# Cross-attention and FFN on one core: FFN rows laid out by DMA in the head, x2 ahead of q's third pair on GpSimd and ahead of q's last sum on VectorE

## The chip, the cores and the metric

One core of one Trainium2 chip. The metric is the device time of one execution of the kernel in microseconds; the profile is of one execution. TensorE multiplies matrices and transposes tiles into PSUM; VectorE, ScalarE and GpSimd work element by element; SyncE and the queues issue DMAs. Each engine works off its own instructions in the order in which they are written and waits on semaphores for the others.

## The reference

The input x has 16 batches of 128 x 1024 (channels x tokens), and so has ctx. Both stages add to x:

```python
def _layernorm(x, axis=-1, eps=1e-05): ...          # over the 1024 tokens
# cross attention, 8 heads of 64, q from layernorm(x), k and v from ctx
qh = softmax(Wq q, axis=-2) * SCALE                 # over the 64 of a head
kh = softmax(Wk k, axis=-1)                         # over the tokens
context = einsum('bhdn,bhen->bhde', kh, vh)
out = Wo (context qh) + bo
x = x + out / max(norm(out), 1e-12) * g * sqrt(128)
# FFN, 4-bit weights: low and high nibble of qweight, per output scale and zero
w = (w_int - round(zeros / scales)) * scales
x = x + layernorm(x) w + bias
```

The result is x after both, in float32.

## The kernel before

The weights are prepared once, then 16 batches go through a software pipeline. `iteration(i, ...)` is written once for every engine; in it, batch n = i + 1 is loaded, normalised and given k's first projection, batch a = i goes through q and k (attention weights), batch c = i - 1 through the attention's output and its norm (up to x2, the sum after the first stage), and batch f = i - 2 through the FFN. Iterations -1 (FIRST) to 2 are peeled, which also hold the set-up, 3 to 14 are a hardware loop with two iterations to a turn (ScalarE's ends earlier), 15 (END) to 17 are peeled again. An iteration has eight steps j. The order of an engine's work is the order of the `if j == ...` lines by hand; nothing is planned at run time.

The names that matter:

- TensorE: `project_q(j)` makes q for 128 tokens in one PSUM bank (three matmuls, `ps_q`), `project_k(b, j)` k for 128 of 512 rows in two banks (`ps_k`), `transpose_k`, `transpose_c` turn k's exponentials and ctx, `mix_m` is k times ctx (fp32), `mix_g` multiplies with the product of Wv and Wo (`vo`), `mix_out(h)` makes the attention output of half h from g and the turned q, `feed_forward` the FFN, whose last matmul adds zero and bias rows from `ffn_rows`. `set_up_cols` and `set_up_row` spread scales, zeros and bias over the partitions by 3 + 24 transposes in iteration 0.
- VectorE: `max_k` (L840, the k maximum), `shift_q` (L847 maximum, L852 shift), `sum_q(a, p)` (L859, L862: sum and reciprocal of the pair p of q's eight slices), `stats2` and its mean (L1046, L1052), `split_g` (L887, L892: g's high and low part), `low_x2`, `attend`, `fit_g`, whose last instruction is `gs_undo` (L879). In the head it also picks the nibbles of the packed weights (`set_up_late`, L830, one per step j of iteration 0) and mixes and splits the rows (L795 to L806) in iteration 1.
- ScalarE: `exp_q`, `exp_k(b, sums, j)` (L558), `high_q(b, p)` (L574, the f16 high part of pair p), `move_m` (L602), `normalise_x2` (L638), `high_x2` (L647), `xn_hi` (L744), `convert_nibble` (L535), `squares`. At step 0 it issues the loads of x_res, x and ctx (L693 to L700).
- GpSimd: `scale_q(b, p)` (L417, L419), `low_q(b, p)` (L429, what is left of q after the high part), `c_lo`, `xn_lo` (L499), the sum x2 (L510), `fit_x2` (L442 to L447: x2's rstd and mean times rstd), `add_y`.
- SyncE: it turns each finished q part and x2 part by DMA transpose, in the order of the code (`turn_q`, L347, L372, L377), each behind a wait.

The FFN's x2 comes into TensorE's layout by the transposes of x2n_hi and x2n_lo. The order around the change: on GpSimd at step 6 `scale_q(a, 2)`, at step 7 `xn_lo`, x2, `low_q(a, 2)`; at step 0 of the next iteration `fit_x2(f)`, `scale_q(c, 3)`, `low_q(c, 3)`. On VectorE at step 7: q's shift, `max_k(n, 0)`, `sum_q(a, 3)`, x2's statistics, k's reciprocal, the mean. On ScalarE at step 0: `move_m`, the load issues, `normalise_x2`, `exp_q(0)`, `high_x2`, `high_q(c, 3)`, `exp_k(a, s, 1)`.

## Time and profile before

| what | value |
| --- | --- |
| time, median of 3 runs | 705.52 us (703.21 to 708.35) |
| the profiled execution | 706.99 us, its span 704.9 us |
| TensorE busy | 654.4 us, 93% of the span |
| VectorE busy | 555.5 us, 79% |
| GpSimd busy | 474.5 us, 67% |
| ScalarE busy | 449.6 us, 64% |
| mean granted TensorE clock | 0.978 |

Times in the rows are us from the start of the span; a line number is that of the code above. A bracket at the end of a timeline row is the idle time of the engine ahead of the instruction and what ended it. TensorE's matmuls overlap, so their durations add up to more than the time between their starts.

### The profile page before, as it was taken

How to read it: one execution, taken by the hardware profiler on the slowest of the kernel's cores; microseconds unless marked ns; L12 is line 12 of the kernel's file. 1: busy time of each engine (PE TensorE's matmuls, PEld its weight loads, DVE VectorE, ACT ScalarE, POOL GpSimd, SP SyncE). 2: the span in 40 equal slices, each digit the busy share in tenths (PEclk: the TensorE clock that was granted, in tenths of full speed). 3: DMA queues.
4: the chain of work that ended last, by engine and by line, in shares of the span. 5: the costliest groups of instructions: out<-in, count | busy, mean ns of one | idle time of the engine just before them, and what ended most of it. 6: DMA issues, size and time to landing. Idle time of an engine off the chain costs nothing.

```text
span 704.9 us, 11155 instructions
## 1 busy us (share of the span) xinstructions
PE 654.4 (93%) x3312; PEld 420.1 (60%) x3328; DVE 555.5 (79%) x900; ACT 449.6 (64%) x747; POOL 474.5 (67%) x406
## 2 busy tenths in 40 slices
PE   4858799999999999999999999999999999999987
PEld 3635556666666666656666666666666665666543
DVE  2997778888878788888878888888878887887844
ACT  3575666767585767667485666758575766748432
POOL 2166286776949496785949677694949678594820
PEclk9989889999999999999999999999999999999989
DMA  8125236363553637263454636255363724344451
GB/s 297 62 52 120 54 54 171 91 152 59 149 113 83 164 89 179 50 173 74 119 126 96 166 89 163 50 154 105 80 161 89 179 53 116 69 114 78 92 106 60
DMA packets 178871, 78.43 MB, mean 111 GB/s; under 512 B 168328, under 2 KB 169888, under 8 KB 178848
## 3 DMA queue, kind: packets, MB, share of 16 engines
q1 hardware_dynamic: 172512, 55.09, 36.9%
q10 hardware_dynamic: 6336, 23.07, 9.7%
q8 instruction: 10, 0.16, 0.1%
q14 instruction: 13, 0.11, 0.1%
HBM read 28.32 MB, written 8.39 MB: 52 GB/s over the span
## 4 chain that ended last, share of the span: by engine, by line
PE 34%; POOL 25%; issue 19%; DVE 12%; ACT 7%; DMA 1%; POOLq 0%; another core or an unknown queue 0%; DVEq 0%; ACTq 0%; SPq 0%
PE ps_m L1268 6%; POOL q_tok_lo L429 6%; POOL x L510 3%; POOL q_exp L419 3%; PE ps_m L1180 3%; POOL c_lo L473 3%; DVE q_sum L859 3%; POOL y L435 3%; PE ps_k L1110 3%; PE ps_o L1110 2%; POOL rn L492 2%; PE ps_k L1112 2%; PE ps_o L1111 2%; PE ps_k L1111 2%; PE ps_o L1112 2%
## 5 line engine op out<-in xcount | busy, mean ns | idle before, releaser
L429 POOL TENSOR_TENSOR q_tok_lo<-q_exp,q_tok_hi 128x1024 f16<-128x1024 f32 x64 | 140.0, 2189 | 85.8 <-ACT q_tok_hi L574 85.8
L419 POOL TENSOR_TENSOR q_exp<-q_exp,q_rec 128x1024 f32<-128x1024 f32 x64 | 122.2, 1910 | 5.0
L1180 PE MATMUL ps_m<-k_t,c_t 128*128 128x512 f32 x256 | 119.8, 602 | 0.0
L563 ACT ACTIVATE q_exp<-q_exp 128x512 f32<-128x512 f32 x128 | 80.5, 629 | 45.9 <-DVE q_exp L852 45.9
L840 DVE TENSOR_REDUCE k_nmax<-ps_k 128x1 f32<-128x1024 f32 x64 | 78.1, 1220 | 40.1 <-PE ps_k L1112 40.0
L558 ACT ACTIVATE k_exp<-ps_k,k_nmax 128x1024 f32<-128x1024 f32 x64 | 71.1, 1110 | 55.1 <-DVE k_nmax L840 55.1
L574 ACT ACTIVATE q_tok_hi<-q_exp 128x1024 f16<-128x1024 f32 x64 | 67.6, 1056 | 49.8 <-POOL q_exp L419 49.8
L847 DVE TENSOR_REDUCE q_nmax<-ps_q 128x8 f32<-128x512 f32 x128 | 87.3, 682 | 11.2 <-PE ps_q L1112 9.6
L852 DVE TENSOR_TENSOR q_exp<-ps_q,q_nmax 128x512 f32<-128x512 f32 x128 | 88.5, 692 | 5.1 <-DVE q_nmax L847 0.2
L1110 PE MATMUL ps_q<-wq_hi,xn_lo 128*128 128x512 f32 x128 | 74.4, 581 | 9.7 <-DVE q_exp L852 7.0
L417 POOL TENSOR_TENSOR q_rec<-q_rec,q_range 128x16 f32<-128x16 f32 x64 | 15.6, 244 | 93.3 <-DVE q_rec L862 93.3
L859 DVE TENSOR_REDUCE q_sum<-q_exp 128x16 f32<-128x1024 f32 x64 | 77.4, 1209 | 0.7 <-ACT q_exp L563 0.7
L1180 PEld LDWEIGHTS ps_m<-k_t,c_t 128*128 128x128 f32 x256 | 47.2, 194 | 41.6 <-issue 40.2
L1110 PE MATMUL ps_k<-c_hi,wk_lo 128*128 128x512 f32 x128 | 64.1, 501 | 8.2 <-ACT k_exp L558 8.1
L1110 PE MATMUL ps_o<-q_hi,g_lo 128*128 128x512 f16 x128 | 50.2, 392 | 9.3 <-issue 5.5
L1268 PE MATMUL ps_m<-w_int,x_hi 128*128 128x512 f16 x224 | 53.1, 380 | 0.0
L1268 PE MATMUL ps_m<-w_int,x_lo 128*128 128x512 f16 x224 | 52.9, 379 | 0.0
L1111 PE MATMUL ps_k<-c_lo,wk_hi 128*128 128x512 f32 x128 | 51.5, 403 | 0.0
L1112 PE MATMUL ps_k<-c_hi,wk_hi 128*128 128x512 f32 x128 | 51.5, 402 | 0.0
L1111 PE MATMUL ps_q<-wq_lo,xn_hi 128*128 128x512 f32 x128 | 51.2, 400 | 0.0
L1112 PE MATMUL ps_q<-wq_hi,xn_hi 128*128 128x512 f32 x128 | 51.0, 399 | 0.0
L1111 PE MATMUL ps_o<-q_lo,g_hi 128*128 128x512 f16 x128 | 50.2, 392 | 0.0
(185 smaller groups left out, 1385.1 us busy)
## 6 DMA issues: line engine op xcount, KB each, us to landing
x_res<-in_x ACTq DMA_DIRECT2D x16, 512.0 KB, 3.4
out_x<-y SPq DMA_DIRECT2D x15, 512.0 KB, 2.9
x_in<-in_x ACTq DMA_DIRECT2D x14, 512.0 KB, 4.7
c_in<-in_ctx ACTq DMA_DIRECT2D x14, 512.0 KB, 6.0
x_in<-in_x SPq DMA_DIRECT2D x2, 512.0 KB, 6.0
c_in<-in_ctx SPq DMA_DIRECT2D x2, 512.0 KB, 8.1
q_hi<-q_tok_hi SPq DMA_TRANSPOSE x64, 3.1
q_lo<-q_tok_lo SPq DMA_TRANSPOSE x64, 3.1
```

The source lines that it names most:

```text
L419: nc.gpsimd.tensor_tensor(pair, pair, rec.unsqueeze(2).to_broadcast([P, 2 * HEADS, DH]), ALU.mult).then_inc(qs_done, 1)
L429: nc.gpsimd.tensor_tensor(q_tok_lo[p % 2][:], q_exp[:, 2 * p:2 * p + 2, :].rearrange("p t d -> p (t d)"), q_tok_hi[p % 2][:], ALU.subtract ...
L563: nc.scalar.activation(q_exp[:, j, :], q_exp[:, j, :], ACT.Exp).then_inc(qexp_done, 1)
L840: nc.vector.tensor_reduce(k_nmax[:, j:j + 1], ps_k[:], op=ALU.max, axis=AX_X, negate=True).then_inc(kmax_done, 1)
L847: nc.vector.tensor_reduce(q_nmax[:, j, :], heads, op=ALU.max, axis=AX_X, negate=True).then_inc(qmax_done, 1)
L852: nc.vector.tensor_tensor(q_exp[:, j, :].rearrange("p (h d) -> p h d", h=HEADS), heads, q_nmax[:, j, :].unsqueeze(2).to_broadcast([P, HEAD ...
L859: nc.vector.tensor_reduce(q_sum[:, two, :], q_exp[:, two, :].rearrange("p t (h d) -> p t h d", h=HEADS), op=ALU.add, axis=AX_X).then_inc(q ...
L1110: nc.tensor.matmul(ps, lhs_lo, rhs_hi, start=start, stop=False)
L1111: nc.tensor.matmul(ps, lhs_hi, rhs_lo, start=False, stop=False)
L1112: return nc.tensor.matmul(ps, lhs_hi, rhs_hi, start=False, stop=stop)
L1180: last = nc.tensor.matmul(ps_m[:], c_t[s][:, t, :], k_t[:, t, :], start=(t == 0), stop=(t == TC - 1))
L1268: nc.tensor.matmul(ps_m[:], (x2_hi, x2_lo)[part][:, k, :], w, start=(part == 0 and k == 0), stop=False)
```

## The change

The FFN's rows: before, scales, zeros and bias go through TensorE's transposes and ScalarE's copies to all partitions and are mixed and split on VectorE and ScalarE in iteration 1. After, scales are spread over the partitions by one DMA; zeros and bias are split into three bf16 parts where they are (8 partitions) and 12 DMAs on SyncE put the parts in their rows of `ffn_rows`, which GpSimd has set to zero. The nibble buffer gets a tile of its own, four of the eight picks and conversions move to iteration 1, and the copies of `vo` go from VectorE to ScalarE. FIRST gets an order of its own on VectorE (x's statistics, ctx's maximum, xn, then the set-up), GpSimd, ScalarE and TensorE.

In every iteration: on GpSimd `scale_q(a, 2)` comes behind xn_lo and x2, and `fit_x2` follows it at once, ahead of `low_q(a, 2)`; on VectorE `sum_q(a, 3)` comes behind x2's statistics and mean; on ScalarE `high_q(c, 2)` moves to step 0 of the next iteration behind `move_m`, and `exp_k(a, s, 1)` goes ahead of `high_q(c, 3)`; `gs_undo` becomes a tensor_scalar.

```diff
-        zero_bc = sb("zero_bc", [P, OUT])
-        bias_bc = sb("bias_bc", [P, OUT])
+        nibble = sb("nibble", [P, OUT])
...
-        row_pick = sb("row_pick", [P, 2])
...
-        q_nibble = [t[:].bitcast(I32) for t in (y, x_res)]
+        q_nibble = [t[:].bitcast(I32) for t in (y, nibble)]
         rows_in = sb("rows_in", [TC, 3, P])
         inv_scale = sb("inv_scale", [TC, P])
-        cols = sb("cols", [P, 3, TC])
+        row_parts = sb("row_parts", [TC, 2, 3, P], BF16)
...
+        NIBBLES = [(m + 2 * late, high) for late in range(2) for high in range(2) for m in range(2)]
...
+            sp.dma_start(scale_bc[:], scales.rearrange("o a -> (a o)").partition_broadcast(P)).then_inc(scale_spread, 16)
+            sp.wait_ge(consts_made, 10)
+            for part in range(3):
+                sp.wait_ge(rows_split, (1, 3, 4)[part])
+                for r in range(4):
+                    row = 32 * part + r
+                    sp.dma_start(ffn_rows[row:row + 1, :].rearrange("a (t c) -> a t c", t=TC),
+                                 row_parts[:, r // 3, part, :]).then_inc(rows_placed, 16)
...
+            nc.gpsimd.memset(ffn_rows[:], 0.0).then_inc(consts_made, 1)
...
+                first = isinstance(i, int) and i == FIRST
+                if first:
+                    fit_x()
+                    low_c()
...
+                if isinstance(i, int) and i == 0:
+                    both = rows_in[:, 1:3, :]
+                    pool.wait_ge(rows_split, 1)
+                    nc.gpsimd.tensor_tensor(both, both, row_parts[:, :, 0, :], ALU.subtract).then_inc(rows_split, 1)
+                    pool.wait_ge(rows_split, 3)
+                    nc.gpsimd.tensor_tensor(row_parts[:, :, 2, :], both, row_parts[:, :, 1, :],
+                                            ALU.subtract).then_inc(rows_split, 1)
                 for j in range(STEPS):
-                    if j == 0 and do_f:
-                        fit_x2(f)
...
-                    if j == 3 and do_n:
...
+                    if j == 3 and do_n and not first:
+                        low_c()
...
-                    if j == 6 and do_n:
...
+                    if j == 6 and do_n and not first:
+                        fit_x()
                     if j == 6 and do_c:
 
                         pool.wait_ge(n2_moved, c + 1)
                         nc.gpsimd.tensor_tensor(rn[:], n2[:], neg_half[:], ALU.pow).then_inc(rn_done, 1)
-                    if j == 6 and do_a:
+                    if j == 6 and isinstance(i, int) and i == END:
...
                             if h == 0:
                                 pool.wait_ge(xres_loaded, 16 * (c + 1))
+                                if isinstance(i, int) and i == 1:
+                                    pool.wait_ge(nibble_done, 2 * RC)
                                 if begun(c):
                                     pool.wait_ge(x2n_done, c)
                             nc.gpsimd.tensor_tensor(halves(x2)[h], halves(og)[h], halves(x_res)[h],
                                                     ALU.add).then_inc(x2_done, 1)
+                    if j == 7 and do_a and not (isinstance(i, int) and i == END):
+                        scale_q(a, 2)
+                    if j == 7 and do_c and not (isinstance(i, int) and i == END):
+                        fit_x2(c)
                     if j == 7 and do_a:
...
+            def move_vo():
+
+                act.wait_ge(vo_ready, 1)
+                for q in range(2):
+                    nc.scalar.activation(vo[:].rearrange("p (k q o) -> p q k o", q=2, o=P)[:, q],
+                                         ps_o[q][:].rearrange("p (k o) -> p k o", k=HC), ACT.Copy).then_inc(vo_moved, 1)
...
+                m, high = NIBBLES[k]
+                nc.scalar.activation(w_int[:, high, m], q_nibble[k % 2], ACT.Copy).then_inc(w_converted, 1)
...
-                    if j == 4 and isinstance(i, int) and i == FIRST:
+                    if j == 4 and first:
+                        high_x()
                         set_up_rest()
+                    if j == 0 and isinstance(i, int) and i == 0:
+                        act.wait_ge(zero_steps, 5)
+                        nc.scalar.activation(row_parts[:, :, 0, :], rows_in[:, 1:3, :], ACT.Copy).then_inc(rows_split, 1)
                     if j == 0 and do_c:
                         move_m()
+                        high_q(c, 2)
...
+                    if j == 0 and do_a:
+                        exp_k(a, s, 1)
...
-                    if j < 3 and do_a:
+                    if 1 <= j < 3 and do_a:
...
-                    if j == 6 and do_n:
...
+                    if j == 6 and do_n and not first:
+                        high_x()
...
-                    if j == 6 and do_a and not (isinstance(i, int) and i == END):
-                        high_q(a, 2)
-                    if isinstance(i, int) and i == 0:
-                        set_up_ffn(j)
-                    if isinstance(i, int) and i == 1 and j == 2:
-                        act.wait_ge(rows_mixed, 2)
-                        nc.scalar.activation(ffn_rows[:], zero_bc[:], ACT.Copy).then_inc(rows_split, 1)
-                    if isinstance(i, int) and i == 1 and j == 4:
+                    if isinstance(i, int) and i == 0 and j == 0:
+                        move_vo()
                         act.wait_ge(rows_split, 2)
-                        nc.scalar.activation(ffn_rows[32:64, :], bias_bc[32:64, :], ACT.Copy)
-                        nc.scalar.activation(ffn_rows[64:96, :], bias_bc[64:96, :], ACT.Copy).then_inc(rows_split, 1)
+                        nc.scalar.activation(row_parts[:, :, 1, :], rows_in[:, 1:3, :], ACT.Copy).then_inc(rows_split, 1)
+                    if isinstance(i, int) and i == 0 and j in (2, 4, 6, 7):
+                        convert_nibble((2, 4, 6, 7).index(j))
                     if isinstance(i, int) and i == 1 and j == 0:
-                        convert_nibble(2 * RC - 1)
-                        act.wait_ge(w_converted, 2 * RC)
                         nc.scalar.dma_start(x_res[:], x[c]).then_inc(xres_loaded, 16)
+                    if isinstance(i, int) and i == 1 and j in (2, 3, 4, 6):
+                        convert_nibble(4 + (2, 3, 4, 6).index(j))
...
-            def set_up_mix():
...
-                dve.wait_ge(rows_moved, 6)
-                dve.wait_ge(pick_done, 2)
-                nc.vector.tensor_scalar(zero_bc[:], zero_bc[:], row_pick[:, 0:1], None, ALU.mult).then_inc(rows_mixed, 1)
-                dve.wait_ge(rows_mixed, 1)
-                nc.vector.scalar_tensor_tensor(out=zero_bc[:], in0=bias_bc[:], scalar=row_pick[:, 1:2], in1=zero_bc[:],
-                                               op0=ALU.mult, op1=ALU.add).then_inc(rows_mixed, 1)
-
-            def set_up_split(k):
-
-                dve.wait_ge(rows_split, 2 * k + 1)
...
+            def pick_nibble(k):
+
+                m, high = NIBBLES[k]
...
+                nc.vector.tensor_scalar(q_nibble[k % 2], q_packed[m], 4 * high, 15, ALU.logical_shift_right,
...
-                    nc.vector.tensor_tensor(gs_undo[:], g_undo[:], gs_col[:], ALU.mult).then_inc(fit_steps, 1)
+                    if isinstance(i, int) and i == 0:
+                        dve.wait_ge(gs_done, 1)
+                    nc.vector.tensor_scalar(gs_undo[:], g_undo[:], gs_col[:], None, ALU.mult).then_inc(fit_steps, 1)
...
+                if isinstance(i, int) and i == FIRST:
+                    stats_x()
+                    mean_x()
+                    abs_c()
+                    norm_x()
+                    set_up()
                     set_up_rows()
+                    top_c()
+                    max_k(n, 0)
+                    return
...
-                            dve.wait_ge(rows_moved, 6)
+                            dve.wait_ge(scale_spread, 16)
...
-                        set_up_late(j)
-                    if isinstance(i, int) and i == 1 and j == 1:
-                        set_up_mix()
-                    if isinstance(i, int) and i == 1 and j in (3, 5):
-                        set_up_split((j - 3) // 2)
+                        if j == 1:
+                            set_up_gains()
+                        elif j == 3:
+                            set_up_top()
+                        if j in (1, 3, 5, 6):
+                            pick_nibble((1, 3, 5, 6).index(j))
+                    if isinstance(i, int) and i == 1 and j in (1, 2, 3, 5):
+                        pick_nibble(4 + (1, 2, 3, 5).index(j))
...
-                    if j == 7 and do_a:
+                    if j == 7 and isinstance(i, int) and i == END:
                         sum_q(a, 3)
-                    if j == 7 and isinstance(i, int) and i == END:
...
+                    if j == 7 and do_a and not (isinstance(i, int) and i == END):
+                        sum_q(a, 3)
...
-            def set_up_cols():
...
-            def set_up_row(k):
...
-                        pe.wait_ge(rows_moved, 6)
+                        pe.wait_ge(vo_moved, 2)
...
-                                    pe.wait_ge(rows_split, 4)
+                                    pe.wait_ge(rows_placed, 16 * 12)
...
-                            set_up_cols()
-                        elif j < 4:
-                            set_up_row(2 * (j - 1))
-                            set_up_row(2 * (j - 1) + 1)
...
+                    if j == 7 and do_n and isinstance(i, int) and i == FIRST:
+                        project_k(n, 0)
...
-                    if j == 7 and do_n:
+                    if j == 7 and do_n and not (isinstance(i, int) and i == FIRST):
```

`low_c`, `fit_x`, `high_x`, `abs_c`, `stats_x`, `mean_x`, `top_c` and `norm_x` are the instructions of before under a name.

## Rows read from the trace of the kernel before

**Rows 1.** Length, then busy us of PE, PEld, DVE, ACT, POOL; PEclk, DMA share, GB/s.

```profile
20.00:60.20 40.20, 31.65 (x150) 21.91 (x150) 34.96 (x54) 26.30 (x42) 17.66 (x13) 0.87 0.21 53
...
60.20:107.20 47.00, 38.16 (x169) 25.18 (x170) 35.40 (x55) 30.36 (x45) 28.00 (x19) 0.85 0.41 84
...
305.70:345.90 40.20, 39.35 (x204) 25.39 (x204) 33.17 (x55) 26.93 (x46) 29.82 (x26) 1.00 0.49 117
```

**Rows 2.** Timeline of TensorE, iterations 8 and 9 (start us, us, engine, line, ...).

```profile
353.59 0.38 PE L1110 MATMUL ps_o<-q_hi,g_lo 128*128 128x512 f16 x1 [0.29 <-issue]
...
356.94 0.50 PE L1110 MATMUL ps_k<-c_hi,wk_lo 128*128 128x512 f32 x1 [0.60 <-ACT k_exp L558]
...
360.08 1.89 PE L1268 MATMUL ps_m<-w_int,x_hi 128*128 128x512 f16 x8
...
394.37 0.38 PE L1110 MATMUL ps_o<-q_hi,g_lo 128*128 128x512 f16 x1 [0.75 <-DVE g_lo L892]
```

**Rows 3.** Timeline of GpSimd, end of iteration 7 into iteration 8.

```profile
342.05 1.91 POOL L419 TENSOR_TENSOR q_exp<-q_exp,q_rec 128x1024 f32<-128x1024 f32 x1
...
343.91 2.40 POOL L499 TENSOR_TENSOR xn_lo<-xn,xn_hi 128x1024 fp32r<-128x1024 f32 x1
...
346.26 2.52 POOL L510 TENSOR_TENSOR x<-og,x_res 128x512 f32<-128x512 f32 x2
...
348.73 2.14 POOL L429 TENSOR_TENSOR q_tok_lo<-q_exp,q_tok_hi 128x1024 f16<-128x1024 f32 x1
...
351.74 0.19 POOL L447 TENSOR_TENSOR nmr<-nm,rstd 128x1 f32<-128x1 f32 x1
```

**Rows 4.** Timeline of ScalarE, the same stretch.

```profile
341.05 1.06 ACT L744 ACTIVATE xn_hi<-xn 128x1024 fp32r<-128x1024 f32 x1 [1.82 <-DVE xn L1025]
...
348.53 0.69 ACT L602 ACTIVATE m_t<-ps_m,g_fit 128x512 f32<-128x512 f32 x1
...
351.97 1.33 ACT L638 ACTIVATE og<-x,nmr,rstd 128x1024 f32<-128x1024 f32 x1 [2.75 <-POOL nmr L447]
...
354.76 1.04 ACT L574 ACTIVATE q_tok_hi<-q_exp 128x1024 f16<-128x1024 f32 x1
...
355.71 1.09 ACT L558 ACTIVATE k_exp<-ps_k,k_nmax 128x1024 f32<-128x1024 f32 x1
```

**Rows 5.** Timeline of VectorE, the same stretch.

```profile
347.02 1.21 DVE L859 TENSOR_REDUCE q_sum<-q_exp 128x16 f32<-128x1024 f32 x1
...
348.43 1.22 DVE L1046 BATCH_NORM_STATS2 stats<-x 128x6 f32<-128x512 f32 x2
...
353.02 1.22 DVE L840 TENSOR_REDUCE k_nmax<-ps_k 128x1 f32<-128x1024 f32 x1
```

**Rows 6.** DMA to landing, of the tiles x2n_hi and q_tok_lo in turn.

```profile
DMA to landing us min/median/max: 3.2/3.3/4.5
...
DMA to landing us min/median/max: 3.0/3.1/7.5
```

**Rows 7.** Timeline of TensorE, the first q of iterations 0 and 1.

```profile
19.90 0.47 PE L1110 MATMUL ps_q<-wq_hi,xn_lo 128*128 128x512 f32 x1 [2.34 <-POOL xn_lo L499]
...
60.18 0.48 PE L1110 MATMUL ps_q<-wq_hi,xn_lo 128*128 128x512 f32 x1 [0.27 <-issue]
```

**Rows 8.** Timeline of VectorE in the head, with waits.

```profile
59.83 0.80 DVE L830 TENSOR_SCALAR x_res<-x 128x1024 int32<-128x1024 int32 x1 [2.51 <-ACT w_int L535]
...
105.24 1.23 DVE L840 TENSOR_REDUCE k_nmax<-ps_k 128x1 f32<-128x1024 f32 x1 [0.51 <-PE ps_k L1112]
```

**Rows 9.** VectorE's q maximum (a group) and gs_undo (ns min/median/max).

```profile
L847 DVE TENSOR_REDUCE q_nmax<-ps_q 128x8 f32<-128x512 f32 x128 | 87.3, 682 | 11.2 <-PE ps_q L1112 9.6 <-issue 1.6
...
L879 DVE TENSOR_TENSOR gs_undo<-g_undo,gs_col x16: 621/1143/2135, 49.0 to 655.3; 128x1 f32<-128x1 f32 x16
```

**Rows 10.** The nibble picks: busy time in iteration 0, one output's durations.

```profile
20.00:60.20 40.20, 7.78 (x8) 0.87 0.21 53
...
L830 DVE TENSOR_SCALAR y<-og x2: 686/1431/2176, 26.2 to 43.5; 128x1024 int32<-128x1024 int32 x2
```

More of the change, by code:

```diff
@@ L559, in exp_k, with high_x @@
                                          accum_out=k_sum[:, sums, j:j + 1]).then_inc(kexp_done, 1)
+                first = isinstance(i, int) and i == FIRST
+                def high_x():
+                    act.wait_ge(xn_done, n + 1)
+                    if begun(8 * a):
+                        act.wait_ge(q_ready, 8 * a)
+                    nc.scalar.activation(xn_hi[1 - s][:], xn[:], ACT.Copy).then_inc(xnhi_done, 1)
                 def exp_q(j):
@@ L995, in iteration @@
                     if j == 5 and do_n:
-                        dve.wait_ge(x_loaded[1 - s], loads(n, 1 - s))
-                        if begun(n):
-                            dve.wait_ge(ve1_done, n)
-                            dve.wait_ge(xn_done, n)
-                        for h in range(HALVES):
-                            nc.vector.bn_stats(stats1[:, h, :], halves(x_in[1 - s])[h]).then_inc(stats1_part, 1)
-                        dve.wait_ge(stats1_part, 2 * (n + 1))
+                        stats_x()
                     if j == 5 and do_a:
@@ L1005, in iteration @@
                     if j == 5 and do_n:
-                        nc.vector.bn_aggr(mv1[:], stats1[:].rearrange("p a b -> p (a b)")).then_inc(stats1_done, 1)
-                    if j == 5 and isinstance(i, int) and i == FIRST:
-                        set_up()
+                        mean_x()
                     if j == 6 and do_c:
@@ L1057, in _ @@
         def _(pe):
-            pe.wait_ge(consts_made, 9)
+            pe.wait_ge(consts_made, 10)
             pe.wait_ge(wqk_loaded, 32)
@@ L1078, in set_up_vo @@
                 last.then_inc(vo_ready, 1)
-            def set_up_cols():
-                pe.wait_ge(zero_steps, 4)
-                for k in range(3):
-                    last = nc.tensor.transpose(ps_m[:, k * TC:(k + 1) * TC], rows_in[:, k, :], ident[0:TC, 0:TC])
-                last.then_inc(cols_ready, 1)
-            def set_up_row(k):
-                if k == 0:
-                    pe.wait_ge(cols_moved, 1)
-                    pe.wait_ge(vo_moved, 2)
-                elif k > 1:
-                    pe.wait_ge(rows_moved, k - 1)
-                for t in range(4):
-                    col = cols[:, k // 2, 4 * (k % 2) + t:4 * (k % 2) + t + 1]
-                    last = nc.tensor.transpose(ps_o[k % 2][:, t * P:(t + 1) * P], col.to_broadcast([P, P]),
-                                               ident[:])
-                last.then_inc(rows_ready, 1)
             def set_up_spread():
-                pe.wait_ge(cols_moved, 1)
                 pe.wait_ge(vabs_done, 1)
```

122 lines of the change are left out of this document (52 added, 70 removed).

## The prediction, made before the change was run

> **What bounds the kernel now.** I read the page's head first, then the busy times by stretch, then TensorE's timeline in one full iteration with the other engines beside it, then the head the same way. The body is a TensorE body: in a full iteration of 40.2 us TensorE is busy for 39.35 us, VectorE for 33.2, GpSimd for 29.8 [rows 1]. Only a wait of TensorE costs anything there. The two iterations of the head are another matter: iteration 0 takes 40.2 us with 31.65 us of TensorE in it and 34.96 of VectorE, iteration 1 takes 47.0 us with 38.16 us of TensorE, at a mean granted clock of 0.87 and 0.85 [rows 1], though neither has the FFN matmuls. There VectorE's long queue, with TensorE and ScalarE waiting on each other between, sets the pace.
>
> In the body TensorE waits in two places [rows 2]. Iteration 8 (from 345.9): 0.29 us ahead of mix_out(0) at 353.59, behind g's low part, and 0.60 us ahead of project_k(2) at 356.94, which waits for ScalarE's second exponential of k. Iteration 9 has 0.75 us ahead of mix_out(0) at 394.37 instead; its q maximum on VectorE starts some 0.6 us later, which I put down to the loop's jump, since it comes in every second iteration.
>
> Why that exponential is late is a chain over GpSimd: q's third pair is scaled at 342.05 (1.91 us), then xn's low part at 343.91, x2 at 346.26, q's low part at 348.73 (2.14 us), and only then the four small steps of x2's rstd, the last at 351.74 [rows 3]. ScalarE waits 2.75 us for it, normalises at 351.97, and runs q's high part of the fourth pair at 354.76 ahead of the exponential at 355.71, 1.09 us long [rows 4].
>
> **The loop, part by part.** GpSimd: xn's low part needs ScalarE's xn_hi, done at 341.05 + 1.06 = 342.1 [rows 4], so it runs 342.2 to 344.55; x2 to 347.05; the third pair's scaling (0.3 + 1.9, its queue behind nothing) to 349.15. VectorE's x2 statistics need x2's halves at 345.8 and 347.05. Without the sum ahead of them they start at 347.02, where the sum stands now, and the second half 0.6 us later [rows 5]: they do not wait, but the cover shrinks from 1.4 us to about 0.5. They end at 348.3 and mean and variance are there by 348.6, so rstd runs on GpSimd 349.2 to 350.25. ScalarE does m_t (348.53, 0.69 us [rows 4]), then q's high part of the third pair, which waits for the scaling: 349.2 to 350.2; then the three load issues. For these I take 1.0 us, between nothing and 2.75, the idle stretch in which they lie now [rows 4]: the normalisation starts at 351.2 instead of 351.97. Only 0.75 us are won there, since high part and issues now stand ahead of it. From its start through q's exponential and x2's high part it is 354.76 - 351.97 = 2.8 us; then the second exponential of k comes at once, q's high part (0.95) now behind it: 354.0, but its k maximum is there only at 353.02 + 1.22 = 354.25 [rows 5]. So 354.4 instead of 355.71, and it ends at 355.5. mix_out(0) ends at 353.59 + 2.77 = 356.35, so the 0.60 us wait goes, with 0.8 us to spare. VectorE's chain from the k maximum to g's low part has the same instructions in another order, so the waits ahead of mix_out(0) (0.29 and 0.75) stay. Late next is that chain.
>
> So even iterations 4 to 14 win 0.6 us each, 3.6; the odd ones, where mix_out(0) itself is late, nearly nothing, 0.1 each, 0.5; iterations 2, 3 and 15 are peeled or first in the loop and I give them 0.6 each, 1.8. Term of the loop: 6 us. Bounds: 0 (the wait returns under another name) and 14 x 0.9 = 12.6 (both waits go everywhere).
>
> gs_undo becomes a tensor-scalar: 1.14 us in the median for one column, up to 2.14 [rows 9]; I put the new form at 0.2, with 0 and 1.14 as its ends. In the loop it stands where TensorE is never idle, so I cost it at nothing; in iteration 0 it gives 1.9 on VectorE's path. If its cover were gone in the loop, it would be worth 1 us per iteration, and a gain.
>
> **The head.** All of it is counted up to the first k maximum of iteration 2, now at 105.24 [rows 8].
> Before iteration 0: x's statistics go ahead of c's maximum, its rstd ahead of c's low part on GpSimd, xn's high part ahead of Wo's turn. xn's low part then ends near 17.0, and TensorE, doing k's first projection and the second half of c's transposes first, starts q at about 17.9 instead of 19.90 [rows 7]. Win 2.0.
> Iteration 0: VectorE loses the two copies of vo (a 128x512 read of PSUM like the q maximum, 0.68 each [rows 9]) to ScalarE, which is idle there, four of eight nibble picks (all eight take 7.8 us; four unhindered ones at 0.7 take 2.8 [rows 10]), 1.9 of gs_undo, and the wait of 2.51 us for ScalarE's conversion at 59.83 [rows 8]. That is 1.4 + 5.0 + 1.9 + 2.5 = 10.8 us. TensorE loses 27 small transposes, ScalarE seven copies and four conversions. Walking VectorE's queue with 1.35 us for each maximum and shift (twice 0.68 [rows 9]), 1.41 for each sum with its reciprocal (347.02 to 348.43 [rows 5]), and TensorE at full clock, I get the last k maximum of iteration 0, which now follows the pick at 59.83, at about 51.5 instead of 60.5; new waits appear for a q exponential that stands behind the second pair's high part on ScalarE (1 us) and for xn's rstd (0.2). q of iteration 1 starts at 53.1 instead of 60.18 [rows 7], after xn's low part, which no longer has the third scaling ahead of it.
> Iteration 1: VectorE loses the two mixing and two splitting passes over 1024 elements (1.21 us each like the q sum's 1024 elements [rows 5]: 4.8) and 0.8 of gs_undo, and gains four picks (2.8). ScalarE loses three copies. Walked on, the k maximum of iteration 2 comes at about 90: 105.24 - 90 = 15.2 us.
> The rows themselves now come over 12 small DMAs on SyncE, behind waits for parts that are ready by 26 in my walk; even at 0.9 us an issue they are out of the queue by 37, before q's first transpose is due near 38; ffn_rows and scale_bc are first used in iteration 2. Nothing.
> The walk has TensorE at full clock, and the trace does not: the clock was lower in both iterations [rows 1]. Gaps of 1 to 2 us remain in my walk too, ahead of q's start, mix_g and project_k(2) of iteration 1. I take 3.2 us off: term of the head 12 us. Bounds: 5 (only VectorE's removed passes of iteration 1 and the 2 us at the start) and 16.
>
>
> Of VectorE's two picks out of og the one at 43.5 took 2.18 us and the other 0.69 [rows 10].
> The Trainium skill ("SBUF — State Buffer", SBUF: two separate sides) says that the port pair which GpSimd shares with VectorE is an exclusive lock, held for a whole instruction. By that rule two picks of the new order, the third of iteration 0 and the last of iteration 1, fall on GpSimd's busy stretches, and the head would give 9 rather than 12, the whole 692 rather than 689; the pick of 2.18 us agrees, since GpSimd computed c's low part beside it.
>
> **Sum.** The profiled execution took 706.99 us, 704.9 of it the span. 706.99 - 12 - 6 = 689. It lies 1.5 us above the median of 705.52; against the median it would be 687.5. I predict 688.5.
>
> **Rivals.**
> Head only (0.14): the loop gives nothing. For it: VectorE's cover of 0.5 us for x2's statistics is thin, and SyncE must now put x2's high transpose right behind q's low one of the third pair (issue near 352.6, then 354.2). Against: the last matmuls due on it start at 360.08, less 0.6 [rows 2], and it lands in 3.3 us [rows 6]. 706.99 - 12 = 695.
> Loop only, with little of the head (0.12): ScalarE and GpSimd pace the head once VectorE is lighter, and the clock stays low. For it: ScalarE has the vo copies ahead of the first turns of k. Against: it was busy for 26 of 40 us. 706.99 - 6 - 5 = 696.
> Neither, within 1% (0.07): 706.99 - 5 = 702 and less.
> Slower (0.05): x2's high transpose becomes the bound. It stands on SyncE behind the transpose of q's third low part, which waits for GpSimd's low part, which now waits for ScalarE's high part, 1.7 us later than now. While the loads run, a q_lo transpose has landed after as much as 7.5 us, where 3.1 is usual [rows 6]. If x2's took 7.5 from 354.2 on, the FFN would start at 361.7, not 360.08: 1.6 us in each of 14 iterations, 22 us, and the head's 12 back: 717. It decides from a landing of about 5.3 us on.
>
> **How the numbers follow.** The forecast holds 0.62; its own range is 684 to 694. To reach 8 in 10 I take in the two half-way cases, up to 698, and the head's full 16 with more of the loop down to 682. About 1% is what a measurement of this kernel can tell. Faster by over 1% (under 698.5): 0.62 + 0.14 + 0.12 less a little of the tails, 0.86. Within 1%: 0.09. Slower: 0.05.
>
> **What would show it.** In the profile after: the wait ahead of project_k(2) for the exponential gone in even iterations, the wait ahead of mix_out(0) still there; the period of two iterations 79.7 instead of 80.4; the first k maximum of iteration 2 near 93; gs_undo at 0.2 us; ScalarE's normalisation 0.7 us earlier relative to the k maximum. I am wrong if VectorE's x2 statistics wait for GpSimd, if the first FFN matmul waits for a transpose, or if the head's gain is outside 5 to 16.

## The result, and the profile after

The changed kernel takes 757.88 us in the median of four executions (752.47 to 763.23), the kernel before on the same chips 704.72: a ratio of 1.074, with a 95% interval of 1.066 to 1.083. I had forecast 688.5, with 698 as the upper end, and gave "slower" one chance in twenty. Everything below takes the profiled execution, whose span is 761.4 us beside 704.9.

The first view is the head of the page of the changed kernel: span, and busy time of each engine.

```profile
span 761.4 us, 11074 instructions
PE 669.9 (88%) x3285; PEld 426.1 (56%) x3301; DVE 545.6 (72%) x893; ACT 446.8 (59%) x741; POOL 472.7 (62%) x409
```

TensorE is busy for 15.5 us more than before (669.9 against 654.4), although the change took work from it, and idle for 41 more. VectorE has less to do and waits more. So TensorE waits for something, and then computes slowly. The groups of instructions name it (busy us, mean ns | idle us ahead of the group, and its releaser), and the profile's list of DMA issues has the suspects (KB, median us from issue to landing). The same FFN matmuls had 53.1 us, 380 ns each and no idle time in the kernel before.

```profile
L1284 PE MATMUL ps_m<-w_int,x_hi 128*128 128x512 f16 x224 | 70.2, 470 | 54.3 <-DMA x_hi<-x2n_hi 54.3
```

```profile
x_in<-in_x ACTq DMA_DIRECT2D x14, 512.0 KB, 5.6
c_in<-in_ctx ACTq DMA_DIRECT2D x14, 512.0 KB, 11.5
x_hi<-x2n_hi SPq DMA_TRANSPOSE x15, 8.7
```

54.3 us of waiting for the transpose of x2's high part, which used to land in 3.3 us [rows 6] and now needs 8.7, and 70.2 - 53.1 = 17.1 us more for the matmuls behind it. Less my 18 us of gains that gives 704.9 + 54.3 + 17.1 - 18 = 758; the span is 761.4. The second number is the clock: in the windows around one such wait (length, busy us of PE, PEld, DVE, ACT, POOL; granted clock, DMA share, GB/s) TensorE has no work from 346 on, and the granted clock falls to the lower of its two levels, 1.2 GHz, and stays there while the FFN begins.

```profile
346.00:348.00 2.00, 0.00 (x0) 0.00 (x0) 1.71 (x3) 1.91 (x6) 0.18 (x1) 1.00 1.07 152
348.00:350.00 2.00, 0.29 (x1) 0.13 (x2) 0.00 (x0) 0.00 (x0) 1.92 (x2) 0.59 1.22 254
350.00:352.00 2.00, 2.00 (x6) 0.75 (x5) 0.00 (x0) 0.00 (x0) 0.02 (x1) 0.50 0.88 187
```

TensorE's timeline shows the wait in iteration after iteration, eleven times; the period is 46.8 us here, where it was 40.2 [rows 1].

```profile
349.71 3.59 PE L1284 MATMUL ps_m<-w_int,x_hi 128*128 128x512 f16 x8 [4.42 <-DMA x_hi<-x2n_hi]
396.47 1.04 PE L1284 MATMUL ps_m<-w_int,x_hi 128*128 128x512 f16 x2 [4.59 <-DMA x_hi<-x2n_hi]
```

What holds the transpose is on SyncE's timeline and on ScalarE's, here in the iteration of that first wait. The second column is how long the issue itself took.

```profile
335.85 1.23 SPq L350 DMA_TRANSPOSE q_hi<-q_tok_hi  x1
338.16 2.76 SPq L350 DMA_TRANSPOSE q_lo<-q_tok_lo  x1
341.01 6.66 SPq L375 DMA_TRANSPOSE x_hi<-x2n_hi  x1
347.77 1.26 SPq L350 DMA_TRANSPOSE q_hi<-q_tok_hi  x1
```

```profile
334.77 1.06 ACT L603 ACTIVATE q_tok_hi<-q_exp 128x1024 f16<-128x1024 f32 x1
335.09 0.34 ACTq L727 DMA_DIRECT2D x_res<-in_x  x1
335.68 0.34 ACTq L730 DMA_DIRECT2D x_in<-in_x  x1
336.26 0.37 ACTq L734 DMA_DIRECT2D c_in<-in_ctx  x1
336.68 1.33 ACT L667 ACTIVATE og<-x,nmr,rstd 128x1024 f32<-128x1024 f32 x1 [0.86 <-issue]
```

x2's high part is ready at 339.6 as I had reckoned, but the issue of q_lo ahead of it lasts 2.76 us instead of 1.23, so its transpose is issued only at 341.01, and that issue lasts 6.66 us instead of 1.23. The transfers of this iteration took, by the trace: q_hi 12.1 us from its issue, c_in 11.7, q_lo 10.6, x_hi 8.7. So q_hi and c_in both land near 347.9, and the other two at 348.8 and 349.7: once under way together, q_hi, q_lo and c_in crawl and end together. x_hi is another case. From the end of its issue it needs 2.0 us, as it did before (3.3 - 1.23 = 2.1); what is long is the issue, and it ends 0.3 us before q_hi lands. The same holds in ten of the eleven iterations with a wait: the issue ends 0.3 to 0.6 us before q_hi's landing (1.9 us in the other).

In the kernel before q's high transpose was over long before the loads (its issue was 3.7 us ahead of the first of them, and the rounding that releases it ended at 345.19), and its low one came 0.9 us after the last load and landed in 5.9:

```profile
345.21 1.23 SPq L347 DMA_TRANSPOSE q_hi<-q_tok_hi  x1
350.90 1.35 SPq L347 DMA_TRANSPOSE q_lo<-q_tok_lo  x1
354.88 1.23 SPq L372 DMA_TRANSPOSE x_hi<-x2n_hi  x1
```

```profile
344.13 1.06 ACT L574 ACTIVATE q_tok_hi<-q_exp 128x1024 f16<-128x1024 f32 x1 [2.02 <-POOL q_exp L419]
348.94 0.34 ACTq L693 DMA_DIRECT2D x_res<-in_x  x1
349.46 0.34 ACTq L696 DMA_DIRECT2D x_in<-in_x  x1
350.04 0.34 ACTq L700 DMA_DIRECT2D c_in<-in_ctx  x1
```

In the changed kernel there were also three iterations of the new order without a wait (the last one, END, keeps the old order). In two of them no x and no context is left to load (q_hi 3.9 and 3.5 us, x_hi 2.9). In the third, all loads are there, but the context's happened to go out 0.12 us ahead of q_hi's transpose, at 611.37 and 611.49: q_hi 7.3 us, x_hi 3.3. In the eleven iterations with a wait it went out 0.23 to 0.79 us behind. That one iteration made me doubt that the mere amount of traffic was the cause.

The steps that I had walked through on the other engines came as forecast: the first k maximum of iteration 2 at 91.99 instead of 105.24, gs_undo in 0.21 us, the wait ahead of project_k(2) for the exponential down from 8.1 us in 11 places to 2.3 in 3.

### The profile page after: what moved, and what is told of

Same layout as the page of the kernel before. It is cut to its first block, busy times and chain, and to the rows that moved or that the text cites. A ratio compares the mean times of both kernels' runs of the same rounds, so it can differ in the third digit from the quotient of the medians.

```text
span 761.4 us, 11074 instructions
## 1 busy us (share of the span) xinstructions
PE 669.9 (88%) x3285; PEld 426.1 (56%) x3301; DVE 545.6 (72%) x893; ACT 446.8 (59%) x741; POOL 472.7 (62%) x409
## 4 chain that ended last, share of the span: by engine, by line
PE 39%; issue 17%; POOL 17%; DVE 10%; DMA 9%; ACT 5%; SPq 2%; another core or an unknown queue 0%; POOLq 0%; ACTq 0%; DVEq 0%
PE ps_m L1284 9%; DMA x_hi<-x2n_hi 7%; POOL q_tok_lo L450 5%; PE ps_m L1197 5%; POOL q_exp L423 3%; POOL x L532 2%; DVE q_sum L866 2%; POOL c_lo L429 2%; PE ps_o L1127 2%; SPq L350 2%; PE ps_k L1127 2%; PE ps_o L1129 2%; PE ps_o L1128 2%; PE ps_k L1128 2%; POOL y L456 2%
## 5 line engine op out<-in xcount | busy, mean ns | idle before, releaser
L450 POOL TENSOR_TENSOR q_tok_lo<-q_exp,q_tok_hi 128x1024 f16<-128x1024 f32 x64 | 137.9, 2156 | 172.9 <-ACT q_tok_hi L603 172.8
L1284 PE MATMUL ps_m<-w_int,x_hi 128*128 128x512 f16 x224 | 70.2, 470 | 54.3 <-DMA x_hi<-x2n_hi 54.3
L1284 PEld LDWEIGHTS ps_m<-w_int,x_hi 128*128 128x128 f16 x224 | 23.1, 113 | 89.6 <-DMA x_hi<-x2n_hi 50.6
L1127 PE MATMUL ps_k<-c_hi,wk_lo 128*128 128x512 f32 x128 | 69.3, 541 | 2.3 <-ACT k_exp L578 2.3
L1128 PE MATMUL ps_k<-c_lo,wk_hi 128*128 128x512 f32 x128 | 53.7, 419 | 0.0
```

Of the source, the lines that this page charges most:

```text
L450: nc.gpsimd.tensor_tensor(q_tok_lo[p % 2][:], q_exp[:, 2 * p:2 * p + 2, :].rearrange("p t d -> p (t d)"), q_tok_hi[p % 2][:], ALU.subtract ...
L1127: nc.tensor.matmul(ps, lhs_lo, rhs_hi, start=start, stop=False)
L1128: nc.tensor.matmul(ps, lhs_hi, rhs_lo, start=False, stop=False)
L1284: nc.tensor.matmul(ps_m[:], (x2_hi, x2_lo)[part][:, k, :], w, start=(part == 0 and k == 0), stop=False)
```

## The experiments

Theory A: the new order of the loop lets q's third high transpose start among the loads of ScalarE, and that slows all of them. Rivals: B, the head's twelve row copies leave SyncE's queue in a bad state; C, three transposes in close succession hold one another, loads or not. The times are medians; ratios are to the kernel before in the same session (704.9 to 706.3 us).

**1. The head alone.**
```diff
+                    if j == 0 and do_f:
+                        fit_x2(f)
...
                         move_m()
-                        high_q(c, 2)
...
-                    if j == 0 and do_a:
-                        exp_k(a, s, 1)
```
and likewise scale_q(a, 2), high_q(a, 2) and sum_q(a, 3) at their places of before.

> The changed kernel with the steady loop's order put back as it was (scale and rounding of q's third pair, x2's rstd, x2's statistics, exp of k's second block at their old places); the head is the new one. Theory A, the loop's new order is what costs (the third pair's high transpose now starts among the loads of x and of the context, and x2's high transpose is held on SyncE behind it): no wait of the first FFN matmul, x2's high transpose issued in 1.23 us, and the head's gain alone, 13 us (the first maximum of k at 91.99 us instead of 105.24): about 692 us. Rival B, the new head's twelve row copies leave SyncE's queue in a worse state for the rest of the run: about 745 to 765 us, with transposes that land in 8 us or more.

694.23 us, ratio 0.984 [0.982, 0.986]. The first k maximum of iteration 2 is at 92.28, no FFN matmul waits, and x2's high transpose lands in 3.2 us. B falls. The head, with gs_undo's new form in it, is worth 11.2 us.

**2. The loop alone**, the same edit the other way round, in the kernel before.

> The kernel before with only the steady loop's new order, its old head. Theory A: the 54 us of waits for x2's high transpose are there again, and the head's 13 us are not gained: about 765 to 775 us, x2's high transpose landing 8 to 12 us after its issue. Rival B (the head's copies spoil the queue): about 699 to 705 us, no such wait.

751.32 us, ratio 1.066 [1.061, 1.070]: 46 us slower than before, without any of the head. The group of the FFN matmuls:

```profile
L1272 PE MATMUL ps_m<-w_int,x_hi 128*128 128x512 f16 x224 | 66.4, 450 | 39.9 <-DMA x_hi<-x2n_hi 39.9
```

I had expected 765 or more, for 54 us of waits; there were 39.9. The mechanism is there; its size varies from run to run, and what sets it within a run stays open. The two halves do not add up either: 46 - 11 = 35 us, and the changed kernel lost 53. Its first two stalls, 5.6 and 8.2 us against 0.8 and 4.7 here, are 8.3 us of that.

**3. Both loads late.** In the changed kernel, the block that issues x_in and c_in moves from step 0 to step 5:
```diff
-                    if j == 0 and (not isinstance(i, int) or 0 <= i < NB - 2):
+                    if j == 5 and (not isinstance(i, int) or 0 <= i < NB - 2):
                         act.wait_ge(xn_done, i + 1)
                         nc.scalar.dma_start(x_in[s][:], x[i + 2]).then_inc(x_loaded[s], 16)
```

> The changed kernel, with ScalarE issuing the loads of the next x and the next context block at its step 5 (before the squares' successors, where SyncE has no transpose under way for some 9 us) instead of at step 0; the load of x for the residual stays where it is. Theory A (the transposes are slowed by loads that run beside them): all transposes of the third pair and x2's high one land in 3 to 4 us as in the last iterations of the changed kernel (3.9, 3.2, 2.9 us), no FFN wait, iterations of 39.3 to 40 us: about 684 us (680 to 690). Rival C (three transposes that follow one another on SyncE within 5 us hold one another, loads or not): the waits stay, about 750 us.

684.75 us, ratio 0.971 [0.969, 0.972]. SyncE's timeline with the three transposes still 2.3 and 1.3 us behind one another:

```profile
374.93 1.23 SPq L350 DMA_TRANSPOSE q_hi<-q_tok_hi  x1
377.24 1.23 SPq L350 DMA_TRANSPOSE q_lo<-q_tok_lo  x1
378.56 1.29 SPq L375 DMA_TRANSPOSE x_hi<-x2n_hi  x1
```

They land in 4.0, 3.1 and 2.8 us. C falls: the close succession alone costs TensorE no wait. The clock is back too; the FFN group and a stretch of two iterations:

```profile
L1284 PE MATMUL ps_m<-w_int,x_hi 128*128 128x512 f16 x224 | 53.0, 379 | 0.0
```

```profile
300.00:380.00 80.00, 78.99 (x413) 51.14 (x412) 66.15 (x109) 55.05 (x91) 59.73 (x51) 1.00 0.50 120
```

The same stretch of the changed kernel had TensorE busy for 71.55 us at a granted clock of 0.91.

**4. Both loads first**, the same block ahead of move_m and high_q(c, 2) in step 0.

> The changed kernel, with the loads of the next x and the next context block issued at the very start of ScalarE's step 0, before the copy of m and the rounding of q's third pair, so that both loads are under way more than 1 us before the third pair's high transpose is issued. If what counts is the order (a load that is issued after a transpose has begun is what makes all of them crawl; in the one iteration of the changed kernel where the context's load went 0.12 us ahead of the transpose that took 7.3 us and x2's 3.3): no FFN wait, about 686 us (682 to 695). If what counts is how many bytes of loads and transposes lie in the same 10 us: waits of 1 to 4 us in most iterations, 715 to 755 us.

684.88 us, ratio 0.971 [0.970, 0.973], with no FFN wait; x2's high transpose in 2.9 us. These loads started well ahead of the transpose (in one iteration 3.1 and 2.5 us: 333.40 and 333.98, against 336.51), so much of them was over; only x_res stayed close, 0.9 us ahead. This run alone does not part order from amount.

**5. Only the context's load late.** Of the block, the c_in part goes to step 5; x_res and x_in stay.

> The changed kernel with only the context block's load moved to ScalarE's step 5; the residual's load and the next x's load stay at step 0, the last of them about 0.2 us ahead of the third pair's high transpose. Order (a load issued after a transpose has begun is what makes them crawl): no load follows the transpose any more, x2's high transpose lands in 3 us, no FFN wait: 685 us (683 to 690). Amount alone (bytes of loads that share the time with transposes; a third of them gone): a high transpose of some 6 to 8 us, waits of 0 to 2 us: 686 to 705 us.

686.98 us, ratio 0.974 [0.970, 0.978]. q_hi lands in 5.2 to 6.6 us and x2's in 3 in all but one iteration with an x load. The one, with 1.5 us of waiting, had q_hi in 8.5 us and x2's high transpose in 6.0; there x_in's issue, at 96.05, lasted 1.31 us and so reached past the start of q_hi's at 96.75.

**6. All loads right before the rounding.** x_res, x_in and c_in between move_m and high_q(c, 2).

> The changed kernel with all three loads issued right before the rounding of q's third pair instead of after it, so that the same loads and the same transposes stand as close as before, but the last load goes about 1 us ahead of the third pair's high transpose. Order: that transpose lands in 5 to 7.5 us and x2's high one in 3 to 4, no FFN wait, 687 us (684 to 695). Amount: the overlap is nearly what it was, waits of 2 to 4 us stay: 720 to 750 us.

697.08 us, ratio 0.987 [0.986, 0.989], 2 us above the range of "order" and far from that of "amount". In the iteration around 380 the last load went 1.7 us ahead of q_hi's transpose; q_hi took 5.2 us, q_lo 3.7, x_hi 2.9, and no FFN matmul waited. The issue times lie ahead of the rounding, which starts 1.42 us after ScalarE's last work:

```profile
380.91 0.34 ACTq L733 DMA_DIRECT2D c_in<-in_ctx  x1
381.52 1.06 ACT L603 ACTIVATE q_tok_hi<-q_exp 128x1024 f16<-128x1024 f32 x1 [1.42 <-issue]
```

So the crawl is gone, but 12 us of run 3's gain with it. They are not lost at k's second exponential: TensorE waits for it for 2.6 us in 3 places here and for 2.3 in 3 in run 3, against 8.1 in 11 before. What differs is VectorE's low part of x2, 2.62 us in the median here and 1.61 in run 3. It now begins 0.35 us behind the start of GpSimd's scaling of q's fourth pair (385.14 to 387.04), in run 3 only 0.24 us ahead of that scaling's end (377.47 to 379.37), and what stands behind it on VectorE comes later:

```profile
385.49 2.63 DVE L946 TENSOR_TENSOR x2n_lo<-og,x2n_hi 128x1024 f16<-128x1024 f32 x1
```

```profile
379.13 1.32 DVE L945 TENSOR_TENSOR x2n_lo<-og,x2n_hi 128x1024 f16<-128x1024 f32 x1
```

Two iterations take 81.1 us instead of 79.3, some 13 us in fourteen. That the overlap with GpSimd makes the pass long was not tested by a run of its own.

**7. The loads behind the normalisation**, in the changed kernel: normalise_x2 moves ahead of the block.

> The changed kernel with the loads of the next x and of the context issued behind the normalisation of x2, so about 1 us after the third pair's high transpose and before its low one. Order: both loads now follow a transpose, and all crawl: waits for x2's high transpose of 4 us or more, 750 to 775 us. Amount: also about 750 us. Against both, if what matters is a load that is issued within half a microsecond of a transpose: no wait, about 690 us.

778.49 us, ratio 1.104 [1.100, 1.109], 59.7 us of waits in all twelve iterations that load a context block: above the 775 us that "order" allowed, and further from the others. ScalarE hands its DMAs over while the normalisation still computes, so the distance that I had wanted did not come about: in one iteration q_hi's transpose started at 332.69, x_in at 332.74, c_in at 333.32. It does show the crawl again, with both loads behind the transpose.

**8. The same edit in the kernel before.**

> The kernel before, whole, with the same edit: the loads of the next x and of the context issued behind the normalisation of x2, so that they go 1 to 2 us after the third pair's low transpose has begun (before: 0.9 us ahead of it) and 1 to 2 us ahead of x2's high one. Order: the old kernel shows the crawl too: both transposes and the context's load land in 7 us or more, waits for x2's high transpose in most iterations, 720 to 745 us. Amount: the two transposes and two loads overlap about as much as before, 705 to 712 us.

705.49 us, ratio 1.000 [0.998, 1.001]. Here the loads went 1.2 and 1.8 us behind q_lo's transpose (350.55; 351.76 and 352.33), and nothing happened: q_lo 3.0 us, x_in 3.6, c_in 4.4, x_hi 3.3. So a load behind a transpose is not bad as such. Either it must fall close to the transpose's start, or other transposes must follow closely.

**9. The kernel before, loads pinned to the transpose.**
```diff
                         act.wait_ge(xn_done, i + 1)
+                        if do_c:
+                            act.wait_ge(qlo_done, 4 * c + 3)
```

> The kernel before, whole, with one wait more: ScalarE issues the loads of the next x and of the context only once the low part of q's third pair is rounded, the event that also starts its low transpose on SyncE. So x's load starts with that transpose and the context's about 0.6 us behind its start, as it stood to the high transpose in the changed kernel; but the transposes keep their old distances (the high one 5.7 us earlier, x2's high one 4 us later). If a load issued just behind a transpose's start is enough: the low transpose, the context's load and x2's high transpose land in 7 to 12 us, waits of 2 to 6 us for the latter, 720 to 760 us. If it also takes the transposes' close succession (q's high and low 2.3 us apart, x2's 2 to 3 us later): no such wait, 704 to 709 us.

708.28 us, ratio 1.006 [1.003, 1.009]: slower by some 3 us. The time is in the second range, some landings are those of the first. With x_in 0 to 0.25 us and c_in 0.5 to 0.8 us behind q_lo's start, q_lo landed in 4.8 to 11.0 us, against about 6 before, and x2's transpose, 4 us later, in 3.3 to 7.6; TensorE's waits ahead of the FFN come to 3.1 us in the profiled execution. So a load at a transpose's start lengthens some landings (the largest was 7.5 before), but with the old distances the jam mostly dissolves in time.

**10. Only x's load late**, the counterpart of run 5: the same bytes stay at step 0, but the last load is one place later.

> The changed kernel with only the next x's load moved to ScalarE's step 5; the residual's load stays ahead of the third pair's high transpose, the context's some 0 to 0.5 us around its start. The same bytes at step 0 as where only the context's load was moved (687 us). If the order decides: the crawl is there in the iterations where the context's load goes behind the transpose's start, so 700 us or more (up to 755), with x2's high transpose landing in 7 us or more. If the bytes decide: as there, 685 to 690 us, no wait.

692.37 us, ratio 0.981 [0.979, 0.984], between the two ranges. In eleven of the twelve iterations that load a context block, this went out 0.03 to 0.62 us ahead of q_hi's transpose: q_hi 5.3 to 7.0 us, no wait. In one it went 0.18 us behind, and only there TensorE waited, for 5.94 us. SyncE's and ScalarE's timeline and TensorE's wait in that iteration:

```profile
136.71 1.24 SPq L350 DMA_TRANSPOSE q_hi<-q_tok_hi  x1
138.94 1.61 SPq L350 DMA_TRANSPOSE q_lo<-q_tok_lo  x1
140.64 7.52 SPq L375 DMA_TRANSPOSE x_hi<-x2n_hi  x1
```

```profile
136.89 0.37 ACTq L735 DMA_DIRECT2D c_in<-in_ctx  x1
```

```profile
151.74 3.59 PE L1285 MATMUL ps_m<-w_int,x_hi 128*128 128x512 f16 x8 [5.94 <-DMA x_hi<-x2n_hi]
```

and SyncE's and ScalarE's rows one iteration later, with the load 0.20 us ahead: the issue of x_hi is back at 1.26 us.

```profile
185.29 1.23 SPq L350 DMA_TRANSPOSE q_hi<-q_tok_hi  x1
187.62 3.15 SPq L350 DMA_TRANSPOSE q_lo<-q_tok_lo  x1
190.85 1.26 SPq L375 DMA_TRANSPOSE x_hi<-x2n_hi  x1
```

```profile
185.09 0.34 ACTq L735 DMA_DIRECT2D c_in<-in_ctx  x1
```

**11. That load pinned behind the start.** One wait more than in run 10, to make the chance a rule:
```diff
+                        if do_c:
+                            act.wait_ge(qhi_done, 4 * c + 3)
                         act.wait_ge(clo_done, i + 1)
```

> The kernel in which only the next x's load stands at step 5, with one wait more: the context's load is issued once the third pair's high part is rounded, the event that starts its transpose too. Against that kernel (692.4 us, one stall of 5.9 us, in the one iteration where the context's load went 0.18 us behind the transpose's start; 0.04 to 0.6 us ahead of it in the others) the load moves by some 0.1 to 0.7 us and nothing else. If a load issued just behind the start is what sets off the crawl: the high transpose in 9 to 13 us, the context's load in 8 to 12, a wait of 3 to 6 us for x2's high transpose in most iterations, 725 to 755 us. If the one stall was of another kind: 690 to 697 us.

727.09 us, ratio 1.030 [1.026, 1.034]. In ten iterations the load now goes 0.22 to 0.37 us behind the transpose (183.16 and 183.39 below); q_hi takes 8.7 to 11.7 us in them, and each has its wait, of 1.1 to 4.5 us (half of them under the 3 that I had expected), 28.3 us in all. In the first and the last of the twelve it went out within 0.01 us of the transpose: q_hi 6.2 and 6.1 us, no wait.

```profile
183.16 1.23 SPq L350 DMA_TRANSPOSE q_hi<-q_tok_hi  x1
185.49 2.15 SPq L350 DMA_TRANSPOSE q_lo<-q_tok_lo  x1
187.72 6.30 SPq L375 DMA_TRANSPOSE x_hi<-x2n_hi  x1
```

```profile
183.39 0.36 ACTq L737 DMA_DIRECT2D c_in<-in_ctx  x1
```

```profile
L1287 PE MATMUL ps_m<-w_int,x_hi 128*128 128x512 f16 x224 | 62.4, 429 | 28.3 <-DMA x_hi<-x2n_hi 28.3
```

35 us between runs 10 and 11, from one load that moved by a few tenths of a microsecond, with the same bytes and the same transposes. 24 iterations of the two runs divide without exception: up to 0.01 us behind the start none waits, from 0.18 us on every one does.

The DMA engines are not idle while they crawl. In run 10, the stretch of the one stall beside a stretch an iteration later in which the load is already through (the last two columns are the DMA engines' share and GB/s):

```profile
142.00:148.00 6.00, 3.80 (x22) 2.80 (x20) 5.08 (x7) 5.74 (x13) 2.16 (x1) 1.00 1.29 89
191.00:194.00 3.00, 3.00 (x19) 2.42 (x17) 2.60 (x4) 2.85 (x9) 2.15 (x1) 1.00 1.24 225
```

Packets of both queues are under way in the first stretch, of SyncE's transposes alone in the second. The packets' time fills the engines in both, but 89 GB/s are moved instead of 225: a transpose's packet takes 99 ns in the mean instead of 22. So in the crawl the two kinds share the engines for long and move little, and the order of the starts decides whether they get there; why it does is not shown.

## Why the prediction was wrong

**The step that failed** is the placing of ScalarE's queue in "the loop, part by part". I wrote that ScalarE does m_t, "then q's high part of the third pair [...]; then the three load issues", and charged the issues with 1.0 us of ScalarE's time. I did not follow what this order does on the DMA side: the rounding's end releases SyncE's transpose, and the load issues then run on beside it. Before, the rounding's end was 3.8 us ahead of the first load (345.19 and 348.94). I took every transpose of the loop at its old landing time of about 3 us, out of a trace in which, up to the last iteration, no load was issued within 1 us behind the start of one. In the last iteration one was (x_res at 669.78, 0.55 us behind q_lo's transpose), and that transpose landed in 5.4 us: a hint that I passed over.

**The rival "Slower"** named the right wait: x2's high transpose as the bound, behind q's third low one while the loads run. Its size was wrong by a factor: I took the worst landing in the old trace, 7.5 us, as its price, and got 1.6 us of waiting an iteration and 717 us in all. Measured were 8.7 us in the median, 54.3 us of waits in eleven iterations (4.9 each) instead of 22, and 17 us at the lower clock, for which I had no term at all. The cause was another, too: I had x2's transpose itself land late, and it was its issue that was held, for 6.8 us in the median of those iterations. What I gave as "against" under "Head only", that the matmuls are due at 360.08, was right about the old landing and empty otherwise. One chance in twenty was too little for a step that moved three DMAs past another queue's.

**The head**, 12 us within 5 to 16: measured 11.2 (run 1). I had the first k maximum of iteration 2 "near 93"; it came at 91.99 in the changed kernel. Of the two picks that I had seen falling on GpSimd's busy stretches, the last of iteration 1 did take 2.47 us instead of 0.68, the third of iteration 0 did not (0.64), and another, at 68.09, took 1.83; the 9 us that I gave by that rule for the head were too low all the same.

**The loop**, 6 us within 0 to 12.6, was right as a term once the transposes keep out of the loads' way: run 1 less run 3 is 694.23 - 684.75 = 9.5 us. Of these, 5.3 are the waits for k's second exponential (7.6 us in run 1, 2.3 in run 3); the rest stands in no single row. The first FFN matmuls of an iteration start at 435.06, 474.94 and 514.33 in run 3, so two iterations take 79.3 us; I had said 79.7. The wait ahead of mix_out(0) for g's low part stayed, as I had said it would: 3.8 us in 5 places before and after. The sum of both terms made 688.5, and run 3 took 684.8.

**gs_undo** at 0.2 us: 0.21. **The row copies** on SyncE cost nothing, as said (run 1). x2's statistics on VectorE did not wait.

**What is shown and what is not.** Shown: the loop's new order is the cause (runs 1, 2); the loads' place beside the transposes is (3 to 6); with bytes and transposes held equal the place of one load's issue, before or behind the start of the transpose, decides (10, 11); and close succession of three transposes without the loads of x and ctx is harmless (3), while loads at a transpose's start without close succession do little (9). Not shown: what happens inside the DMA engines. Not tried: the loads between q_hi's and q_lo's issue with more than a microsecond to both, the same loads issued on SyncE's own queue, and fewer bytes in a load.

**The version that beats both kernels** is run 3 or run 4, 684.8 and 684.9 us: the changed kernel with one block of two loads moved.

## What to carry to other kernels

When an instruction is moved past DMA issues, draw both queues on one time line: which transfers will newly start within a microsecond of each other, on whatever engine they are issued. A landing time read from a trace is valid for the neighbours that it had there, so price a transfer with new neighbours from several times its usual landing, not from its worst old one. Look at the length of the issues on SyncE too: a transfer that lands late may only have been issued late. Long plain loads belong where no transpose is about to start; here they are used a whole iteration later, so that issuing them five steps later cost nothing, and moving them turned 7% lost into 3% won.

## What the runs showed of the hardware

- Transfers that overlapped ended together: in the iteration of 335 us, q_hi, c_in, q_lo and x_hi began 5.2 us apart and all ended between 347.9 and 349.7. With the loads' issue ahead of the transposes (run 6) each of them landed in 3 to 7 us. The Trainium skill ("DMA: Bandwidth & Descriptors", Queues, rings and completion order) says that each DMA engine takes turns, packet by packet, between the queues that have work for it, and that the write of a completion semaphore waits for every earlier write of that engine, across its queues. The common end near 347.9 of a SyncE transpose and a ScalarE load agrees with the second.
- With three transposes in close succession the border is sharp. Counting the load's own issue (0.34 to 0.37 us, longer where something holds it), no iteration of runs 5, 10 and 11 waited in which it was over by 0.39 us behind the start of q's high transpose, and all did in which it ended 0.55 us behind or later. The one of run 5 fits: its load started 0.70 us ahead, but its issue lasted 1.31, to 0.61 us behind. The changed kernel and runs 2 and 7 agree: the last load's issue ended 0.55 to 1.27 us behind the start in 33 iterations, all with a wait of 1.4 us or more, and 0.24 us behind or less in three, where x2's transpose landed in 3.3 us.
- The issue of a DMA can itself be the wait: 6.66 us on SyncE for the third transpose, 1.23 us otherwise. Everything behind it on that queue is late too, and no semaphore wait shows it. The Trainium skill ("Perfetto Trace Analysis", DMA Instruction — HWDGE) says that the profiled time of a DMA's issue takes in a lock wait and the use of the descriptor generator, and not the moving of the data. The 6.66 us agree with an issue that is held. In all 22 waiting iterations of the changed kernel and runs 10 and 11 it ended shortly before the first of the three transposes landed (0.3 to 0.6 us, once 1.9); no run tells what links the two.
- ScalarE issues DMAs while its previous activation still computes: in run 7 the loads went out at 332.74 and 333.32, inside the normalisation from 332.57 to 333.87 (1.30 us). Order in the program is not distance in time.
- The waits were paid again in part by the granted clock, which fell to 1.2 GHz behind one of 4.42 us: 54.3 us of waits brought 17.1 us more of FFN matmuls; in run 11 it was 28.3 and 62.4 - 53.0 = 9.4.
